# Vision-text block with table mean and expert routing on one core: text rows split, table sums by transfers, first expert rows by matmuls

## The reference, cut to what matters

```python
h = concatenate([patches(x) @ proj_w + proj_b + pos_embed, txt], axis=1)
xn = layernorm(layernorm(h), ln_w)                 # attention reads this
avg_wte = mean(wte, axis=0)                        # a table of 50257 x 192
Q = xn[:, None] * W_qk[None, :, None]              # 12 heads, keys are queries
attn = softmax(where(causal, Q @ Q.T / sqrt(192), -inf))
out = (attn @ (xn - avg_wte)) / arange(1, 165)     # per row
h = h + out.reshape(..., 12 * 192) @ W_o.T
y = layernorm(h); n = rmsnorm(y) * ln_w            # expert layer
e = argmax(softmax(n @ w_router))                  # 16 experts, at most 64 rows of a batch each
h = h + y + router_prob * where(routed, relu(n @ wi[e]) @ wo[e], n)
```

## Time and profile before

| | |
|---|---|
| median of 3 runs | 368.05 us |
| lowest, highest | 366.1, 369.53 us |
| the profiled execution's own time | 367.87 us |
| its span | 366.0 us |
| busy: PE, PEld, DVE, ACT, POOL | 334.5, 306.0, 228.0, 126.2, 167.7 us |
| mean granted TensorE clock | 0.967 |

### The profile page before, as it was taken

How to read it: one execution, slowest core, us unless ns; L and a number is a source line. 1 busy time by engine, 2 the same in 40 slices (tenths; PEclk the granted TensorE clock), 3 DMA queues, 4 the chain that set the end, 5 groups by cost and what they waited for, 6 DMA issues and landing times.

```text
span 366.0 us, 6697 instructions
## 1 busy us (share of the span) xinstructions
PE 334.5 (91%) x2336; PEld 306.0 (84%) x2336; DVE 228.0 (62%) x557; ACT 126.2 (34%) x437; POOL 167.7 (46%) x180
## 2 busy tenths in 40 slices
PE   8499969899999999999998979999949999999992
PEld 3388859799899898997997969999815999999991
DVE  0669768789688787796888977657485222222221
ACT  2056543552545436534545024446610111111110
POOL 3173943755854846657548011250661134444321
PEclk9969989999999999999999978999998999999997
DMA  8899999289999995799997969400232699999940
GB/s 252 264 430 282 260 247 217 77 170 230 219 232 230 196 239 143 139 236 270 246 211 199 324 191 289 112 2 1 100 107 73 183 293 266 266 264 260 266 118 17
DMA packets 21096, 74.29 MB, mean 203 GB/s; under 512 B 3540, under 2 KB 9173, under 8 KB 20306
## 3 DMA queue, kind: packets, MB, share of 16 engines
q1 hardware_dynamic: 11362, 43.16, 38.5%
q0 software_dynamic: 6800, 27.82, 37.0%
q10 hardware_dynamic: 2912, 3.04, 3.0%
HBM read 66.12 MB, written 9.25 MB: 206 GB/s over the span
## 4 chain that ended last, share of the span: by engine, by line
PE 66%; DVE 13%; DMA 8%; ACT 5%; issue 5%; ACTq 1%; POOL 0%; POOLq 0%; DVEq 0%
PE bO L1224 18%; PE bS L1224 15%; PE bE L1224 14%; PE bJ L1224 12%; DMA wx<-in_wte 6%; ACT PB L563 2%; DMA hB<-in_txtB 2%; PE bT L1311 2%; DVE wx L856 1%; PE bT L1576 1%; DVE wbuf L856 1%; PE bT L1317 1%; PE bT L1270 1%; DVE oTA L823 1%; ACT pay L620 1%
## 5 line engine op out<-in xcount | busy, mean ns | idle before, releaser
L423 POOL TENSOR_TENSOR PA<-PA,rn 128x512 f32<-128x512 f32 x24 | 25.4, 1057 | 81.5 <-DVE rn L813 81.5
L401 POOL TENSOR_TENSOR AwA<-zT,w 96x512 f32<-96x512 f32 x45 | 50.1, 1192 | 17.4 <-ACT zT L540 17.4
L1224 PE MATMUL bJ<-wo_sb,oTA 128*128 128x192 f32 x288 | 52.7, 333 | 0.0
L558 ACT ACTIVATE PA<-bS,negmax 128x128 f32<-128x128 f32 x96 | 34.0, 367 | 51.3 <-DVE negmax L801 51.2
L1224 PEld LDWEIGHTS bS<-zT,AwA 96*128 96x128 f32 x384 | 47.3, 194 | 1.3 <-issue 0.2
L1224 PEld LDWEIGHTS bJ<-wo_sb,oTA 128*128 128x128 f32 x288 | 47.4, 194 | 0.0
L1224 PE MATMUL bS<-zT,AwA 96*128 96x128 f32 x384 | 47.1, 276 | 0.0
L1224 PE MATMUL bO<-PA,wx 96*128 96x112 f32 x384 | 45.4, 275 | 0.5 <-DVE PA L1197 0.5
L1224 PEld LDWEIGHTS bO<-PA,wx 96*128 96x128 f32 x384 | 44.9, 192 | 0.7 <-DVE PA L1197 0.7
L468 POOL DMA_INDIRECT out<-PA,yrow x16 | 15.1, 942 | 56.0 <-DVE PA L1213 56.0
L695 ACT ACTIVATE AwA<-bO 128x448 f32<-128x448 f32 x16 | 8.7, 544 | 78.5 <-PE bO L1224 52.9
(11 more groups left out here) (252 smaller groups left out, 705.5 us busy)
## 6 DMA issues: line engine op xcount, KB each, us to landing
wbuf<-in_wte POOLq DMA_DIRECT2D x10, 1344.0 KB, 12.7
wx<-in_wte POOLq DMA_DIRECT2D x8, 1344.0 KB, 12.0
wx<-in_wi SPq DMA_DIRECT2D x16, 576.0 KB
wx<-in_wo SPq DMA_DIRECT2D x16, 576.0 KB
wx<-in_wte SPq DMA_DIRECT2D x12, 672.0 KB, 9.2
dispatched<-zeros SPq DMA_DIRECT2D x7, 675.5 KB, 9.0
wbuf<-in_wte SPq DMA_DIRECT2D x2, 1344.0 KB, 7.0
wx<-in_wte SPq DMA_DIRECT2D x2, 1344.0 KB, 17.6
```

The lines of the kernel that those rows point to most:

```text
L401: nc.gpsimd.tensor_tensor(o, zT[:, k, ss].unsqueeze(1).to_broadcast(list(o.shape)), w2[:, k, hs].unsqueeze(2).to_broadcast(list(o.shape)), ...
L423: nc.gpsimd.tensor_tensor(t, t, q.unsqueeze(2).to_broadcast(list(t.shape)), ALU.mult).then_inc(p_ready, 1)
L558: last = nc.scalar.activation(PA[:, h, :], bank[:, j * SA:(j + 1) * SA], ACT.Exp, bias=negmax[:, h:h + 1], accum_out=lsum[:, h:h + 1])
L1224: return nc.tensor.matmul(o, l, r, start=start, stop=stop, skip_group_check=True)
```

## The change

**Start.** Text rows come in two parts: batches 0 and 1 first, the other six behind. VectorE prepares `w2` first, takes `hB`'s statistics of batches 0 and 1 only, and those of the rest after it has begun batch 0. The factors of batch 1 stand before the wait for `zT`. In iteration 0 the variances of batches 2 to 7 and the router weights (`wr_sb`) are formed earlier, and only one part of `plain_sum` stands before `t_low(0, 3)`; the second stands behind `row_max(1, 1)`.

**Table.** `slot_add` is gone. GpSimd issues three transfers (`fold`), which add slot 3 to slot 2, slot 1 to slot 0, and slot 2 to slot 0. VectorE sums the plain halves before, and waits for all three transfers in `table_total`.

**First two blocks.** VectorE makes 0/1 matrices (`select`) that say which row of a tile goes to which of the first 224 places; TensorE multiplies the normalised rows with them (`dispatch`), which gives the transposed rows of blocks 0 and 1 in `bT[1]`. The scatter and the loads stay, since the blocks' sums read them. The rows that no expert takes are formed in three parts around block 0.

```diff
@@ sync
+            for b0, b1, arrived in ((0, 2, txt_in), (2, NBATCH, txt2_in)):
+                for p0, p1 in ((IMG, 116), (116, 128)):
+                    sp.dma_start(H[p0:p1, b0:b1, :], txtA[p0 - IMG:p1 - IMG, b0:b1]).then_inc(arrived, 16)
...
             for s in range(WBUF):
                 sp.wait_ge(wte_in[s], slot_loads(s))
+            sp.wait_ge(fold_in, 16 * 3)
             sp.wait_ge(zero_ready, 1)
@@ gpsimd
+            def fold(s, t, before):
+
+                for w in (s, t):
+                    pool.wait_ge(wte_in[w], slot_loads(w))
+                if before:
+                    pool.wait_ge(fold_in, 16 * before)
+                pool.dma_start(wchunk[s], wchunk[t], accum_op=ALU.add,
+                               max_dma_last_dim=WR * EMB * 4 // 2).then_inc(fold_in, 16)
...
+                if folds:
+                    fold(2, 3, 0)
+                    fold(0, 1, 0)
                 weigh(b + 1, n, (0, 1), (0,))
                 normalise(b, range(3, SPR))
                 weigh(b + 1, n, (0, 1), (1,))
...
                 weigh(b + 1, n, (0, 1), (2,))
+                if folds:
+                    fold(0, 2, 2)
                 normalise(b + 1, (0,))
...
-            iteration(NBATCH - 2)
+            iteration(NBATCH - 2, (), True)
@@ scalar
-            act.dma_start(cst[:], cst_d).then_inc(cst_in, 16)
+            act.dma_start(hB[:, 0:2, :], txtB[:, 0:2]).then_inc(hb_in, 16)
...
-            act.dma_start(hB[:], txtB).then_inc(hb_in, 16)
+            act.dma_start(cst[:], cst_d).then_inc(cst_in, 16)
+            act.dma_start(hB[:, 2:NBATCH, :], txtB[:, 2:NBATCH]).then_inc(hb2_in, 16)
...
-                if h == 3:
+                if h == 7:
                     emb_copy(1)
@@ vector
-            def slot_add(s, t):
...
+            def plain_total():
+
+                dve.wait_ge(plain_used, 4 * WPLAIN)
+                p = psums
+                link(nc.vector.tensor_tensor(chunk_rows(p, 0, 6), chunk_rows(p, 0, 6), chunk_rows(p, 6, 12), ALU.add))
+                link(nc.vector.tensor_tensor(chunk_rows(p, 0, 3), chunk_rows(p, 0, 3), chunk_rows(p, 3, 6), ALU.add))
...
                 dve.wait_ge(wtail_in, 16)
                 w, p = wchunk[0], psums
...
+                dve.wait_ge(fold_in, 16 * 3)
                 link(nc.vector.tensor_tensor(chunk_rows(w, 0, 7), chunk_rows(w, 0, 7), chunk_rows(w, 7, 14), ALU.add))
...
+            def select(B):
+
+                k0, k1 = STAGE[B]
+                link(nc.vector.tensor_tensor(part(posG, B), part(drop, B), part(posF, B), ALU.add))
+                for j0, j1, sel in sels:
+                    lo, hi = max(j0, k0), min(j1, k1)
+                    if lo < hi:
+                        bc = [128, hi - lo, NPE * T]
+                        nc.vector.tensor_tensor(sel[:, lo - j0:hi - j0, :], cst2[:, C_IO:C_IO + NPE * T].unsqueeze(1).to_broadcast(bc),
+                                                posG[:, lo:hi].unsqueeze(2).to_broadcast(bc), ALU.is_equal).then_inc(sel_ready, 1)
...
-            slot_add(2, 3)
-            slot_add(0, 1)
-            slot_add(0, 2)
+            plain_total()
+            table_total()
             residual_b(0)
-            table_total()
             residual_b(1)
...
+            select(0)
             residual_b(2)
...
             place(1)
+            select(1)
...
+                if start:
+                    xt_copy(1, 1)
+                    dropped_rows()
+                else:
+                    xt_copy(b + 1)
@@ tensor
-            stay_warm(bJ, 3)
+            def dispatch(k0, k1):
+
+                for j in range(k0, k1):
+                    j0, _, sel = sels[j >= 10]
+                    for k in range(2):
+                        last = mm(bT[1][0:EC, k * NPE * T:(k + 1) * NPE * T], norm[:, j, k * EC:(k + 1) * EC], sel[:, j - j0, :],
+                                  j == 0 and k == 0, j == SLOTS - 1)
+                return last
+
+            pe.wait_ge(sel_ready, 1)
+            pe.wait_ge(cen_ready, STAGE[0][1])
+            dispatch(0, 3)
...
-            stay_warm(bJ, 10)
+            dispatch(3, STAGE[0][1])
+            stay_warm(bJ, 2)
+            pe.wait_ge(sel_ready, 3)
+            pe.wait_ge(cen_ready, SLOTS)
+            dispatch(STAGE[0][1], SLOTS).then_inc(xT_sum, 1)
             pe.wait_ge(be_ready, 1)
...
-            stay_warm(bJ, 26)
...
-            x_transpose(0, 16)
```

More of the change, by code:

```diff
@@ L333, in _ @@
             sp.wait_ge(scattered, 16 * SLOTS)
-            for q in range(XBUF - 1):
+            for q in (0, 1, 2):
                 rows(sp, q, q)
@@ L699, in block_step @@
                 hidden(b)
-                if not (is0(i) and q == 0):
+                if is0(i) and q == 0:
+                    act.wait_ge(scattered, 16 * SLOTS)
+                else:
                     act.wait_ge(y_ready, b)
@@ L918, in iteration @@
                 e_copy(b, 1)
+                if is0(b):
+                    dve.wait_ge(late_in, 16 * 5)
+                    nc.vector.memset(oneX[:], 1.0)
+                    nc.vector.tensor_tensor(wr_sb[:, :, :], wr_sb[:, :, :], flc[:, :].unsqueeze(2).to_broadcast([EC, 2, EXP]),
+                                            ALU.mult).then_inc(wr_ready, 1)
                 e_copy(b, 2)
-                if is0(b):
-                    variances(2, NBATCH)
                 if not is0(b):
@@ L926, in iteration @@
                     plain_sum(b, 0)
-                plain_sum(b, 1)
+                else:
+                    plain_sum(b, 1)
                 t_low(b, 3)
@@ L1591, in block_step @@
                 last.then_inc(h1_sum, 1)
-                x_transpose((q + 1) % XBUF, (i + 1 + (q + 1) // XBUF) * 16)
+                start = is0(i) and q == 0
+                if not start:
+                    x_transpose((q + 1) % XBUF, (i + 1 + (q + 1) // XBUF) * 16)
                 pe.wait_ge(wox_in[q], turn)
                 pe.wait_ge(h0_ready, b + 1)
-                if not (is0(i) and q == 0):
+                if not start:
                     pe.wait_ge(y_ready, b)
```

112 lines of the change are left out of this document (64 added, 48 removed).

## The result

The changed kernel takes 384.38 us (median of 4 runs, 382.57 to 385.11), beside 367.6 us of the kernel before on the same chip: 1.0446 times as long, 95% interval 1.0384 to 1.0508. The sign was forecast, the size wasn't: 375.8 was predicted, 381 was the upper end. The profiled execution took 384.34, with a span of 382.4, 16.4 us more than the span of before.

The account below looks back on a forecast made before the run. TensorE was taken as busy nearly everywhere, so only its standstills or removable work could give time. 367.87 + 2.5 (start) + 9.1 (table) - 3.7 (first blocks) = 375.8 us; range 363.5 to 381.

Parts of the forecast that it names:

- The sign: Whole kernel: the change makes it slower by over 1%, chance 0.58.
- the half lands 4.8 us later: Start: earlier GpSimd adds halve the loads' speed, so the plain load's first half lands at 52.6 instead of 47.8.
- the 1.05 us of `wr_sb`: Start: forming the router weights where VectorE waits anyway takes 1.05 us, memset included, off the path between iterations.
- the clock's fall before block 0: First blocks, rival: the clock falls or `dropped_rows` comes too late, the term is -1, total 378.5; chance 0.12.
- +9.1: Table: three dependent adding transfers let TensorE go on at 224.0 instead of 214.86, 9.1 us later.
- Start, +2.5 predicted: Start: 4.8 us of load delay less 1.24 and 1.05 us for two moved pieces; ends -2.3 and +4.
- `plain_sum`'s 1.24: Start: moving one of two `plain_sum` parts behind `row_max(1, 1)` takes 1.24 us off the path.
- The 6.4 us vanish: Start: batch 0's scores begin 6.4 us earlier, but this only lengthens TensorE's wait for the plain load.
- The bound of 6 us for the slip, and of -2.3 for no slip: Start: plain load delayed at most 6 us, or not at all (term -2.3, total 371.0, chance 0.12).
- The 9.5 that I took for the third: Table: the third transfer between slots takes 9.5 us from issue to landing, 209.6 to 219.1.
- The rival of fast transfers: Table: transfers between slots run near plain-load speed, term +0.2 instead of +9.1, total 366.9; chance 0.20.
- Blocks, -3.7 predicted: First blocks: the first product begins at 277.8 instead of 281.51, -3.7 us; ends -5 and -1.

Follow-up runs that it names:

- vec_behind: Changed kernel with slots added by VectorE and GpSimd's first two adds moved behind its weighing and a wait for the plain half: 354.49 us, ratio 0.9618 to before.
- before_behind: Kernel before with one edit, GpSimd's first two adds behind its weighing and a wait for the plain half: 363.14 us, ratio 0.9848 to before.
- copies: Changed kernel with the three transfers between slots as plain copies instead of adding ones: 374.36 us, ratio 1.0180 to before.
- vec_folds: Changed kernel with the table part alone undone, the slots added by VectorE again: 368.80 us, ratio 1.0024 to before.
- blocks_only: Kernel before with only the selection of the first two blocks' rows by matmuls and what comes with it: 366.12 us, ratio 0.9909 to before.
- one_fold: Changed kernel with GpSimd's first two adds behind two normalisations, one slot sum by transfer and two on VectorE: 361.37 us, ratio 0.9789 to before.
- warm_gap: Changed kernel with 8 warming matmuls filling TensorE's gap before block 0's first product: 380.01 us, ratio 1.0318 to before.
- fold_behind: Changed kernel with GpSimd's first two adds behind the plain half, one slot sum by transfer and two on VectorE: 349.06 us, ratio 0.9475 to before.
- all_good: fold_behind plus the block count read behind the first product, 4 warming matmuls before it, dropped rows spread over three blocks: 345.80 us, ratio 0.9381 to before.
- held_adds: Changed kernel with GpSimd's first two adds issued behind two normalisations of batch 0, near 28 us: 376.34 us, ratio 1.0200 to before.

## Why the prediction was wrong

Three terms of the sum were too small. The start: "the half lands 4.8 us later" was 6.7, and the 1.05 us of `wr_sb` didn't show. The first blocks: the clock's fall before block 0 had a chance of 0.12 and no place in the sum, and cost 3.1 us. The table: +9.1 was +10.5. The mechanisms named for start and table are the ones that the runs show.

**Start, +2.5 predicted, +5.5 in the trace.** The mechanism was right: scores before 18.5, adds near 20, and a first plain sum that comes late. The term mis-sized is "the half lands 4.8 us later": 54.47 is 6.7 later than 47.79. I took half of the engines' time for all that was left of the loads. The engines take turns by packets: the loads get 53% from 24 to 32 us, where their packets are large, and 18% from 40 to 48, where those just ahead of the plain half are small. Of the two gifts, `plain_sum`'s 1.24 is there (`value(0, 3)` comes 2.79 us after the sum begins, not 3.98). `wr_sb`'s 1.05 is eaten up: TensorE, after its wait, is at 1.2 GHz for longer than before, which costs 0.9 us by the start of the next scores (64.04 beside 57.69, where `value(0, 3)` was 5.5 apart). These are the stretches of the kernel before, then those of the changed kernel:

```profile
51.70:54.70 3.00, 2.93 (x10) 0.50 1.03 231
54.70:57.70 3.00, 3.00 (x23) 0.99 1.04 269
...
57.20:60.20 3.00, 2.94 (x10) 0.50 0.17 18
60.20:63.20 3.00, 3.00 (x17) 0.69 0.93 242
```

**"The 6.4 us vanish".** True of the changed kernel, and too readily taken as a fact of the loads. That all loads together could be early if the adds were not in their way was the same reading of the same rows, and I asked only what the adds would cost more, not what they cost already. The bound of 6 us for the slip, and of -2.3 for no slip, both kept the adds in place; with them away `value(0, 3)` comes over 10 us earlier (before 51.77, vec_behind 41.08), 3.0 of them without the changed start (before_behind 48.73).

**Table, +9.1 predicted, +10.5 in the trace, +12.0 alone.** The chain of three was right. The 9.5 that I took for the third from issue to landing was 9.8. The last add of the table, issued at 189.85, landed 11.6 us later, near 201.5: 5.7 us after the 195.8 taken, the start's slip. The second took 13.4, since the first was still under way, and landed near 215.4, 0.3 later than 209.6 with the start's 5.5. GpSimd issued the third 0.6 us behind that, where I had no time between. These three make up most of the 1.3. The clock isn't in this term: TensorE comes back at the lower level after 13.1 us, but it did so after 2.67 us in the kernel before, and the way from `wte_mean` (214.86 and 230.82) to the last transposed row tile is 49.0 us in both; its rows in the two timelines:

```profile
263.89 0.42 PE L1442 MATMUL bO<-cst,H 128*96 128x128 f32 x2
...
279.81 0.42 PE L1509 MATMUL bO<-cst,H 128*96 128x128 f32 x2
```

The rival of fast transfers is out by copies: plain ones would have been fast, adding ones are not.

**Blocks, -3.7 predicted.** The first product came 3.7 us earlier to the hundredth, but that is luck. TensorE stood still for 2.65 us and not for the 1.7 of the working, because VectorE began the copy to `xT` at 291.90, 0.9 us after the last selection had ended and not at once as in copies; why is open. Without that the gain is 4.5, as in copies, where the way from `wte_mean` to the last row tile took the same. `dropped_rows` fitted only because block 0 was slow: in the six profiles with the whole block at the upper clock and the edit as it is (vec_folds, copies, blocks_only, one_fold, vec_behind, warm_gap) block 1 takes 5.1 us instead of 4.8. The other case, to which I had given 0.12, came as well: the clock fell, and block 0 cost 3.1 us more. The net is -0.6. Seen from the result, it should have had half the chance: of ten profiles with this gap (1.75 to 1.79 us, the changed kernel's 2.65) it fell in five.

**The sum.** The misses have one sign: start 3.0, table 1.3, clock at block 0 3.1, the end 1.1. That is 8.5, and 375.8 + 8.5 = 384.3. The start's 5.5 lay outside its bound of +4, the other two were inside a bound or a rival, and the range added none of the ends together.

**Open.** The parts alone, by their ratios, are 3.6 + 11.9 - 3.3 = 12.2 us, the whole is 16.4. What makes up the 4.2 is not shown: the intervals allow about 2 us for each, and the clock at block 0, some 3 us when it falls, differs from run to run. Why the same gap costs the clock in some executions and not in others was not found.

## What to carry to other kernels

Before an early start is counted as lost or won, look at which transfers it sets free: a load that something waits for should be through before the first transfer that nothing waits for is issued. The test is to move that issue behind a wait on the load's semaphore; here the later place was enough, and the wait never held. A sum moved from an engine to adding transfers pays where one transfer lies beside the engine's other sums, and costs the whole chain where each waits for the last. Gaps of TensorE in front of dense work are worth filling even when they are under 2 us long, if filling them delays nothing: that rests on three profiles without a fall beside five of ten with one.

## What the runs showed of the hardware that I had not expected

- Transfer engines share by packets, not by bytes: 277 packets of 1.7 KB and 274 of 5.1 KB in 8 us, and the small ones' queue moved a quarter of all bytes.
- An adding transfer of 1.376 MB between places of SBUF takes 9.8 us alone, the same bytes copied 6.0 to 6.5.
- TensorE's clock fell to 1.2 GHz at block 0 in five of ten profiled executions after 1.76 to 2.65 us of standing still, and in none of three where warming matmuls filled the gap. That is few: if filling did nothing and the clock fell in half of all executions, three without a fall would come once in eight times.
- Behind the wait for the table (2.66 to 14.63 us) the clock was at 1.2 GHz for some microseconds in all fourteen traces that have the wait, the kernel before among them (0.50 from 215.9 to 221), and the way from `wte_mean` to the last transposed row tile took 47.5 to 49.1 us. In the three without it (one_fold, fold_behind, all_good) the clock stayed up and the same way took 46.5.
- The blocks' transfers have little room: in vec_folds' profile the blocks from the ninth on lost 3.4 us to loads that came late, in held_adds' 2.5, in warm_gap's 2.1, in the changed kernel's 0.8, in the others nothing.
